# Cross-attention scores in TensorE's two row halves, from two fp32r parts, in a post-norm decoder kernel

## Chip, cores and metric

The kernel runs on one core of one Trainium2 chip. The metric is device time in microseconds for one execution, the median of the runs shown.

## What is computed

There are 64 batches of 128 tokens with 512 features. Each goes through self attention (16 heads of 32, rotary positions, causal mask), cross attention and a linear layer on fp8-quantised rows, each followed by a residual sum and a layer norm. Cross attention is the part that changes. It attends over features: its 8 heads split the 128 tokens into groups of 16, and each head has 512 x 512 scores over a contraction of only 16.

```python
def xattn(q, k, v):                       # q = x, k = v = context, each (64, 128, 512)
    qh = q.reshape(b * 8, 16, 512)
    kh = k.reshape(b * 8, 16, 512)
    vh = v.reshape(b * 8, 16, 512)
    qk = jnp.einsum('bdm,bdn->bmn', qh, kh) / sqrt(16)
    ret = jnp.einsum('bmn,bcn->bcm', softmax(qk), vh)
x = layernorm(x + self_attn(x))
x = layernorm(x + xattn(x, context, context))
x = layernorm(x + quantised(x) @ quantised(weight).T)
```

## The kernel before

Each batch passes six stages, and up to six batches are under way at once. The order of all steps on each engine in one slot (one batch's worth of steps) is written out by hand in five tables: `SP_STEPS`, `POOL_STEPS`, `ACT_STEPS`, `DVE_STEPS`, `PE_STEPS`. An entry `cross_scores:23@4` means step `cross_scores`, number 23, for the batch that is at stage 4. Each engine runs its table once a slot in that order, waits on semaphores where a step needs another engine, and never reorders steps. The tables unroll to 69 slots, with the middle ones in a loop over two slots.

A linear layer (`proj_q`, `proj_k`, `proj_v`, `proj_o`, `ffn`; L872) multiplies two fp32r parts of the input with two fp32r parts of the weights, three products of 128 rows by 512 columns in each of four chunks. ScalarE makes the high part `lin_h`, VectorE the low part `lin_l`.

Cross scores are computed twice. `cross_scores` (L985) writes a head's 128 x 512 block of scores with queries in rows into `mx`; VectorE's `cross_max` (L715) takes the negative row maximum. When 16 maxima of four heads (a group) are there, `cross_shift` splits them, `cross_shift_T` (L991) turns them, ScalarE copies them, and two small DMAs put them as rows 96 and 97 into `qst`. Then `cross_scores_T` (L1002) writes the block with keys in rows and with the maximum already subtracted into `st`, ScalarE's `probs` (L559) takes the exponential into `pp`, and `cross_pv` (L1014) multiplies it with the values of four heads, one in each 32-column group of the array, in plain fp32. `mx` and `st` have two banks each, used in turn, so TensorE can fill one while the other is read.

For precision, a head's 16 contraction rows are laid out several times. The query is split in two fp16 parts, the context in three bf16 parts, and five products of parts are stacked: 80 rows, padded with zeros to 96. ScalarE and GpSimd make the parts (`query_high`, `query_low`, `context_high`, `context_rest`), SyncE stores them to HBM (`st_qpl`, `st_kpl`) and loads them back head by head (`ld_qst`, `ld_kst`, five DMAs for each group of four heads).

A batch has 32 `cross_scores` and 32 `cross_scores_T`, one for each head and each block of 128. Three further PSUM banks serve all other products in turns (`BANK`).

## Time and profile before

| | before |
|---|---|
| median of 3 runs | 3355.27 us (3353.78 to 3358.29) |
| profiled execution: span from first to last instruction | 3353.3 us |
| TensorE busy | 3148.0 us, 94% |
| VectorE busy | 2792.0 us, 83% |
| ScalarE busy | 2093.1 us, 62% |
| GpSimd busy | 1251.8 us, 37% |
| moved by DMA | 220.66 MB, mean 66 GB/s |

The page gives the span as the profiled execution's own time and nothing that lies around it. PE is TensorE's matmuls, PEld its weight loads, DVE VectorE, ACT ScalarE, POOL GpSimd, SP SyncE.
### The profile page before, as it was taken

What the parts mean: (1) busy time and instruction counts of PE and PEld (TensorE: products, weight loads), DVE (VectorE), ACT (ScalarE), POOL (GpSimd) and SP (SyncE); (2) the same over time, 40 slices, a digit from 0 to 9 for tenths busy, and PEclk for the clock granted to TensorE, in tenths of its full rate; (3) what the DMA queues carried; (4) which work ended last, traced back from release to release, by engine and by line L of the source; (5) the groups of instructions that cost most, each with busy time, mean ns of one, the idle gap of its engine ahead of it and who ended that gap; (6) DMA issues with size and microseconds to landing.
All of it is one profiled execution on the core that took longest, in us unless ns stands there. A gap on an engine that the chain in (4) does not pass through costs nothing.

```text
span 3353.3 us, 79176 instructions
## 1 busy us (share of the span) xinstructions
PE 3148.0 (94%) x22224; PEld 1676.5 (50%) x22224; DVE 2792.0 (83%) x5187; ACT 2093.1 (62%) x3905; POOL 1251.8 (37%) x1623
## 2 busy tenths in 40 slices
PE   1689999999999999999999999999999999999986
PEld 1445555555555555555555555555555555555432
DVE  6368888888888888888888888888888888888874
ACT  0346666666676666666667666666666766666653
POOL 3223334334343333433433333343343433334321
PEclk9789999999999999999999999999999999999997
DMA  2022222222222222222222122222222222222220
GB/s 75 26 62 74 71 67 71 63 72 65 70 73 64 72 64 66 71 63 73 64 70 73 63 71 66 66 71 63 71 66 70 73 63 71 65 66 71 67 64 17
DMA packets 203973, 220.66 MB, mean 66 GB/s; under 512 B 37760, under 2 KB 160640, under 8 KB 203776
## 3 DMA queue, kind: packets, MB, share of 16 engines
q1 hardware_dynamic: 203776, 218.77, 21.4%
q14 instruction: 163, 1.34, 0.1%
q8 instruction: 34, 0.56, 0.1%
HBM read 141.57 MB, written 77.07 MB: 65 GB/s over the span
## 4 chain that ended last, share of the span: by engine, by line
PE 75%; DVE 14%; issue 7%; POOL 2%; ACT 1%; DVEq 1%; DMA 1%; SPq 0%; POOLq 0%; ACTq 0%
PE bank L872 19%; PE mx L985 14%; PE st L1002 13%; PE pv L1014 12%; PE bank L865 5%; PE bank L907 3%; DVE nm L715 3%; PE bank L956 3%; DVE st L776 2%; PE bank L939 2%; PE bank L959 2%; DVE lin_l L743 1%; DVE yout L838 1%; PE bank L923 1%; PE bank L920 1%
## 5 line engine op out<-in xcount | busy, mean ns | idle before, releaser
L715 DVE TENSOR_REDUCE nm<-mx 128x1 f32<-128x512 f32 x2048 | 1355.0, 685 | 219.9 <-PE mx L985 210.2
L559 ACT ACTIVATE pp<-st 128x512 f32<-128x512 f32 x2048 | 1153.0, 597 | 400.9 <-PE st L1002 385.1
L985 PE MATMUL mx<-kst,qst 96*128 96x512 bf16 x2048 | 765.4, 387 | 29.2 <-DVE nm L715 28.8
L1002 PE MATMUL st<-qst,kst 98*128 98x512 f16 x2048 | 739.6, 387 | 6.9 <-DMA qst<-cross_shift 2.6
L1014 PE MATMUL pv<-pp,vT 128*32 128x512 f32 x4096 | 551.2, 610 | 0.0
L985 PEld LDWEIGHTS mx<-kst,qst 96*128 96x128 f16 x2048 | 189.1, 98 | 445.5 <-DVE nm L715 283.1
L872 PE MATMUL bank<-w_h,lin_h 128*128 128x512 f32 x768 | 394.0, 513 | 4.5 <-DVE lin_l L743 4.4
L1002 PEld LDWEIGHTS st<-qst,kst 98*128 98x128 bf16 x2048 | 190.7, 98 | 317.8 <-ACT pp L559 216.6
L490 POOL TENSOR_SCALAR rstd<-mv 128x1 f32<-128x1 f32 x192 | 36.9, 192 | 817.2 <-DVE mv L779 812.1
L872 PE MATMUL bank<-w_l,lin_h 128*128 128x512 f32 x768 | 306.0, 398 | 0.0
L872 PE MATMUL bank<-w_h,lin_l 128*128 128x512 f32 x768 | 305.0, 397 | 0.0
L500 POOL TENSOR_TENSOR qkn<-ropeA,qkn 128x512 f16<-128x512 f32 x128 | 148.4, 1159 | 397.2 <-ACT qkn L581 391.4
L763 DVE RECIPROCAL o<-bank 128x128 f32<-128x128 f32 x256 | 217.1, 910 | 42.8 <-PE bank L959 42.7
L506 POOL TENSOR_SCALAR_AFFINE_SELECT p<-p 128x512 f32<-128x512 f32 x256 | 163.4, 638 | 197.8 <-ACT p L616 197.7
L496 POOL TENSOR_TENSOR ropeA<-ropeA,ropeB 128x512 f32<-128x512 f32 x128 | 163.7, 1279 | 144.9 <-DVE ropeB L755 144.9
L574 ACT ACTIVATE junk<-bank 128x512 bf16<-128x512 f32 x128 | 76.1, 594 | 203.3 <-PE bank L872 203.3
L616 ACT ACTIVATE p<-bank 128x512 f32<-128x512 f32 x256 | 152.6, 596 | 56.1 <-PE bank L939 47.4
L729 DVE TENSOR_REDUCE nm<-bank 128x4 f32<-128x512 f32 x256 | 174.6, 683 | 10.4 <-PE bank L923 10.3
L568 ACT ACTIVATE lin_h<-bank 128x512 fp32r<-128x512 f32 x64 | 38.2, 597 | 221.1 <-PE bank L865 221.1
L907 PE MATMUL bank<-ident,qkn 128*96 128x128 f16 x2048 | 161.9, 223 | 14.4 <-DVE o L763 7.2
L872 PEld LDWEIGHTS bank<-w_h,lin_h 128*128 128x128 f32 x768 | 149.4, 195 | 44.8 <-DVE lin_l L743 5.9
L907 PEld LDWEIGHTS bank<-ident,qkn 128*96 128x96 f16 x2048 | 146.0, 125 | 48.4 <-issue 19.3
(131 smaller groups left out, 5417.6 us busy)
## 6 DMA issues: line engine op xcount, KB each, us to landing
qst<-q_planes SPq DMA_DIRECT2D x640, 64.0 KB, 2.2
kst<-k_planes SPq DMA_DIRECT2D x640, 64.0 KB, 2.2
k_planes<-kpl SPq DMA_DIRECT2D x64, 384.0 KB, 2.6
xb<-x SPq DMA_DIRECT2D x64, 256.0 KB, 2.7
cx<-ctx SPq DMA_DIRECT2D x64, 256.0 KB, 3.3
q_planes<-qpl SPq DMA_DIRECT2D x64, 256.0 KB, 2.2
x_rows<-x SPq DMA_DIRECT2D x64, 256.0 KB, 2.1
x<-x_rows SPq DMA_DIRECT2D x64, 256.0 KB, 2.7
```

The lines of the kernel that those rows point to most:

```text
L496: g_.tensor_tensor(ropeA[:], ropeA[:], ropeB[:], ALU.add).then_inc(s_rope, 1)
L506: g_.affine_select(out=p1[c % 2][:], in_=p1[c % 2][:], compare_op=ALU.is_ge, fill=0.0, base=0, pattern=[[0, HC], [1, P]], channel_multipli ...
L559: a.activation(pp[:, unit % 2, j, :], st[n % 2][:], ACT.Exp, scale=CROSS_SCALE).then_inc(st_free, 1)
L715: v.tensor_reduce(nm2[:, n // 16, n % 16:n % 16 + 1], mx[n % 2][:], AX.X, ALU.max, negate=True)\
L729: v.tensor_reduce(nm1[:, HC * c:HC * (c + 1)], at(f"s1m{c}")[:].rearrange("p (h k) -> p h k", h=HC), AX.X, ALU.max, negate=True).then_inc( ...
L763: v.reciprocal(o1[:, cols], at("pvs")[:, cols]).then_inc(done, 1)
L865: last = t.transpose(dst[:, c * P:(c + 1) * P], src(c), idm[:])
L872: last = t.matmul(at(name)[:], a[:, rows], w[:, part, cols], start=(part == 0 and i == 0), stop=(part == KC - 1 and i == 2))
L907: last = t.transpose(at(name)[0:SROWS, h * P // 2:(h + 1) * P // 2].bitcast(F16), qkn[k][:, 8 * (i % 2) + h, :, :].rearrange("p g d -> p ( ...
L985: t.matmul(mx[n % 2][:], qst[b.i][0:XROWS, h, c * P:(c + 1) * P], kst[b.i][0:XROWS, h, :], start=True, stop=True).then_inc(mx_full, 1)
L1002: t.matmul(st[n % 2][:], kst[b.i][:, h, i * P:(i + 1) * P], qst[b.i][:, h, :], start=True, stop=True).then_inc(st_full, 1)
L1014: last = t.matmul(pv[32 * j:32 * j + 2 * XD, :], vT[b.i][:, i, GH * g + j, :], pp[:, unit % 2, j, :], start=(i == 0), stop=(i == KC - 1))
```

## The change

Query and context are now both split into two fp32r parts, and three products of parts are stacked: 48 rows for a head. `qst` and `kst` have 128 rows: one head of a pair stands in rows 0 to 47 (two shift rows at 48 and 49), the next in rows 64 to 111 (shift rows 112 and 113). `cross_scores` and `cross_scores_T` are 16 steps each instead of 32, and each issues two matmuls, one for each half of the array's rows, into the two banks of `mx` or `st`. One reduction and one exponential read both banks, 1024 elements. There is one `mx` and one `st` now, not two in turn. The scaling of the maxima goes, the shifts and their transpose are fp32r and fp32, `context_rest` becomes one subtraction, the planes in HBM are 4 bytes wide, the loads are six DMAs a group, and the ones beside the values take one column in place of 16. All five tables and the assignment of banks are new. Since `ffn`, `proj_q` and `proj_o` follow each other in another order, the steps that write `lin_h` wait until the linear layer before has been multiplied (`linear_before`).

```diff
+    ROW_TILE, PAIRS = 64, XH // 2
     NEG = -1e30
     SROWS = 3 * HD
-    XROWS = 96
-
-    Q_PLANE, K_PLANE = (0, 0, 0, 1, 1), (0, 1, 2, 0, 1)
-    N_SC = XH * KC
+    Q_PLANE, K_PLANE = (0, 0, 1), (0, 1, 0)
+    XROWS = len(Q_PLANE) * XD
+    PG = PAIRS // GROUPS
+    N_SC = PAIRS * KC
...
-        qpl = sb("qpl", [P, 2, D], F16)
-        kpl = sb("kpl", [P, 3, D], BF16)
-        qst = [sb(f"qst{i}", [XROWS + 2, XH, D], F16) for i in range(2)]
-        kst = [sb(f"kst{i}", [XROWS + 2, XH, D], BF16) for i in range(2)]
-        vT = [sb(f"vT{i}", [P, KC, XH, 2 * XD]) for i in range(2)]
+        qpl = sb("qpl", [P, 2, D], F32R)
+        kpl = sb("kpl", [P, 2, D], F32R)
+        qst = [sb(f"qst{i}", [P, PAIRS, D], F32R) for i in range(2)]
+        kst = [sb(f"kst{i}", [P, PAIRS, D], F32R) for i in range(2)]
+        vT = [sb(f"vT{i}", [P, KC, XH, XD + 1]) for i in range(2)]
...
-        st = [bank(f"st{i}") for i in range(2)]
+        st = es.enter_context(nc.psum_tensor("st", [P, 2, 512], F32))
         pv = bank("pv")
-        mx = [bank(f"mx{i}") for i in range(2)]
+        mx = es.enter_context(nc.psum_tensor("mx", [P, 2, 512], F32))
         banks = [bank(f"bank{i}") for i in range(3)]
...
         DVE_STEPS = steps("""
+            cross_max:6@4 cross_max:7@4 layernorm:2@6 cross_shift:0@4 cross_norm:0@5 cross_max:8@4
+            self_recip:0@2 self_recip:1@2 cross_max:9@4 self_recip:2@2 self_recip:3@2
+            self_norm:0@2 cross_max:10@4 oT_low:0@2 cross_norm:1@5 cross_max:11@4 add_cross:0@5
+            cross_max:12@4 layernorm:1@5 quant_scale:0@5 cross_max:13@4 self_max:0@1
+            quant_magic:0@5 add_self:0@2 cross_max:14@4 self_max:1@1 self_max:2@1 cross_max:15@4
+            self_max:3@1 xdT_low:0@5 layernorm:0@2 self_shift:0@1 cross_max:0@3 cross_shift:1@4
+            xT_low:0@0 cross_max:1@3 add_ffn:0@5 cross_max:2@3 cross_max:3@3 rope_terms:0@0
+            cross_max:4@3 cross_max:5@3 rope_terms:1@0""")
...
         PE_STEPS = steps("""
-            proj_o:3@2 context_T:0@3 cross_scores_T:5@4 cross_scores_T:6@4 cross_pv:0@4
-            cross_scores_T:7@4 parts_T:3@1 cross_scores_T:8@4 cross_scores:23@4 self_scores:0@1
-            cross_scores_T:9@4 cross_pv:1@4 cross_scores_T:10@4 cross_scores:24@4 cross_scores:25@4
-            cross_scores_T:11@4 self_scores:1@1 cross_scores_T:12@4 cross_scores:26@4 self_scores:2@1
-            cross_scores:27@4 cross_scores_T:13@4 cross_scores_T:14@4 cross_scores:28@4 quant_T:0@5
-            cross_scores:29@4 cross_scores_T:15@4 cross_pv:2@4 cross_scores:30@4 cross_scores:31@4
-            ffn:0@5 ffn:1@5 ffn:2@5 ffn:3@5 x_T:0@0 cross_shift_T:1@4 cross_scores:0@3 cross_pv:3@4
-            self_scores:3@1 cross_scores:1@3 proj_q:0@0 proj_q:1@0 proj_q:2@0 proj_q:3@0
-            cross_scores:2@3 proj_k:0@0 proj_k:1@0 self_shift_T:0@1 proj_k:2@0 cross_scores:3@3
-            proj_k:3@0 cross_scores_T:16@4 cross_scores:4@3 proj_v:0@0 cross_scores_T:17@4
-            cross_scores:5@3 cross_scores_T:18@4 cross_scores:6@3 proj_v:1@0 cross_scores:7@3
-            proj_v:2@0 cross_scores:8@3 cross_scores_T:19@4 cross_scores:9@3 cross_scores_T:20@4
-            proj_v:3@0 self_scores_T:0@1 cross_pv:4@4 cross_scores:10@3 self_scores_T:1@1
-            cross_scores_T:21@4 cross_scores:11@3 cross_scores_T:22@4 self_scores_T:2@1
-            cross_scores:12@3 self_pv:0@1 cross_scores:13@3 cross_scores_T:23@4 self_pv:1@1
-            self_scores_T:3@1 cross_scores:14@3 cross_scores_T:24@4 cross_scores:15@3
-            cross_scores_T:25@4 self_pv:2@1 parts_T:0@0 self_pv:3@1 cross_scores_T:26@4
-            cross_scores_T:27@4 cross_pv:5@4 cross_shift_T:0@3 cross_scores_T:28@4 cross_scores_T:29@4
-            group_T:0@4 cross_scores_T:30@4 cross_scores:16@3 cross_scores_T:31@4 cross_pv:6@4
-            cross_scores:17@3 cross_pv:7@4 cross_scores:18@3 cross_scores:19@3 parts_T:1@0 group_T:1@4
-            proj_o:0@1 cross_scores:20@3 cross_scores_T:0@3 cross_scores_T:1@3 back_T:0@4 parts_T:2@0
-            proj_o:1@1 cross_scores_T:2@3 cross_scores:21@3 proj_o:2@1 cross_scores_T:3@3
-            cross_scores:22@3 cross_scores_T:4@3""")
+            group_T:1@5 cross_scores:11@4 back_T:0@5 context_T:0@3 cross_scores_T:0@4 parts_T:1@1
+            parts_T:2@1 cross_scores:12@4 proj_o:0@2 proj_o:1@2 cross_scores_T:1@4 proj_o:2@2
+            cross_scores:13@4 cross_scores_T:2@4 self_scores:0@1 proj_o:3@2 parts_T:3@1
+            cross_scores_T:3@4 cross_pv:0@4 self_scores:1@1 cross_scores:14@4 self_scores:2@1
+            cross_scores_T:4@4 cross_pv:1@4 self_scores:3@1 cross_scores:15@4 cross_scores_T:5@4
+            quant_T:0@5 cross_scores_T:6@4 cross_scores:0@3 x_T:0@0 ffn:0@5 ffn:1@5
+            self_shift_T:0@1 ffn:2@5 ffn:3@5 cross_scores:1@3 cross_scores_T:7@4 cross_shift_T:1@4
+            cross_pv:2@4 proj_q:0@0 proj_q:1@0 cross_scores:2@3 proj_q:2@0 proj_q:3@0
+            self_scores_T:0@1 proj_k:0@0 cross_scores:3@3 cross_pv:3@4 cross_scores_T:8@4
+            proj_k:1@0 cross_scores:4@3 proj_k:2@0 proj_k:3@0 cross_scores_T:9@4 self_scores_T:1@1
+            proj_v:0@0 cross_scores:5@3 proj_v:1@0 proj_v:2@0 proj_v:3@0 cross_scores_T:10@4
+            self_scores_T:2@1 cross_scores:6@3 cross_pv:4@4 self_pv:0@1 cross_scores_T:11@4
+            self_pv:1@1 cross_scores:7@3 self_scores_T:3@1 cross_scores_T:12@4 group_T:0@4
+            cross_scores:8@3 self_pv:2@1 cross_scores_T:13@4 self_pv:3@1 cross_shift_T:0@3
+            cross_pv:5@4 cross_scores_T:14@4 cross_scores:9@3 parts_T:0@0 cross_scores_T:15@4
+            cross_pv:6@4 cross_scores:10@3 cross_pv:7@4""")
...
+        def linear_before(name, b):
+
+            opens = [(i, stage, turn) for i, (step, k, stage) in enumerate(PE_STEPS) if k == 0
+                     for first, turn in LINEARS if step == first]
+            own = [turn for _, _, turn in opens].index(name)
+            for back in range(1, len(opens) + 1):
+                _, stage, turn = opens[own - back]
+                ahead = opens[own][1] - stage - (back > own)
+                if b.rnd is not None or 0 <= b.b + ahead < BATCH:
+                    return [full(turn, b, ahead)]
+            return []
...
-                    sp.dma_start(kst[b.i][r * XD:(r + 1) * XD, GH * g:GH * (g + 1), :],
-                                 kpl_d[b.idx()][K_PLANE[r]][GH * g * XD:GH * (g + 1) * XD, :]
-                                 .rearrange("(h d) n -> d h n", d=XD)).then_inc(d_kst[b.i][g], 16)
+                for q in range(2):
+                    for r in range(3):
+                        row = ROW_TILE * q + r * XD
+                        sp.dma_start(kst[b.i][row:row + XD, PG * g:PG * (g + 1), :].bitcast(F32),
+                                     kpl_d[b.idx()][K_PLANE[r]].rearrange("(p q d) n -> q d p n", q=2, d=XD)
+                                     [q][:, PG * g:PG * (g + 1), :]).then_inc(d_kst[b.i][g], 16)
...
+            def context_low(b, _):
+                pool.wait_ge(s_kh, b.n(1, 1))
+                g_.tensor_tensor(kpl[:, 1, :], cx[:], kpl[:, 0, :].bitcast(F32), ALU.subtract).then_inc(s_kl, 1)
...
             def probs(b, n):
 
-                unit, j = n // GH, n % GH
+                unit, j = n // PG, 2 * (n % PG)
                 act.wait_ge(st_full, b.n(N_SC, n + 1))
                 act.wait_ge(pv_unit, b.n(UNITS, unit - 1))
-                a.activation(pp[:, unit % 2, j, :], st[n % 2][:], ACT.Exp, scale=CROSS_SCALE).then_inc(st_free, 1)
+                a.activation(pp[:, unit % 2, j:j + 2, :], st[:], ACT.Exp, scale=CROSS_SCALE).then_inc(st_free, 1)
...
             def xT_high(b, _):
+                for point in linear_before("v", b):
+                    act.wait_ge(*point)
                 act.wait_ge(*full("xT", b))
...
             def cross_max(b, n):
                 dve.wait_ge(mx_full, b.n(N_SC, n + 1))
-                v.tensor_reduce(nm2[:, n // 16, n % 16:n % 16 + 1], mx[n % 2][:], AX.X, ALU.max, negate=True)\
-                 .then_inc(mx_free, 1)
+                p, c = n // KC, n % KC
+                out2 = nm2[:, p // PG, :].rearrange("m (q l c) -> m q l c", q=2, l=PG)[:, :, p % PG, c]
+                v.tensor_reduce(out2, mx[:], AX.X, ALU.max, negate=True).then_inc(mx_free, 1)
 
             def cross_shift(b, g):
 
-                dve.wait_ge(mx_free, b.n(N_SC, 16 * (g + 1)))
-                v.tensor_scalar(nm2[:, g, :], nm2[:, g, :], 1.0 / SHIFT_UNIT, None, ALU.mult).then_inc(s_sc2, 1)
-                dve.wait_ge(s_sc2, b.n(GROUPS, g + 1))
+                dve.wait_ge(mx_free, b.n(N_SC, N_SC // GROUPS * (g + 1)))
                 v.tensor_copy(sh2[:, g, 0, :], nm2[:, g, :]).then_inc(s_h2, 1)
                 dve.wait_ge(s_h2, b.n(GROUPS, g + 1))
-                v.tensor_tensor(sh2[:, g, 1, :], nm2[:, g, :], sh2[:, g, 0, :], ALU.subtract).then_inc(s_sh2, 1)
+                v.tensor_tensor(sh2[:, g, 1, :], nm2[:, g, :], sh2[:, g, 0, :].bitcast(F32), ALU.subtract)\
+                 .then_inc(s_sh2, 1)
...
             def cross_scores(b, n):
 
-                h, c = n // KC, n % KC
-                if n % (GH * KC) == 0:
-                    pe.wait_ge(d_kst[b.i][h // GH], b.n2(80, 80))
-                    pe.wait_ge(d_qst[b.i][h // GH], b.n2(80, 80))
-                pe.wait_ge(mx_free, b.n(N_SC, n - 1))
-                t.matmul(mx[n % 2][:], qst[b.i][0:XROWS, h, c * P:(c + 1) * P], kst[b.i][0:XROWS, h, :],
-                         start=True, stop=True).then_inc(mx_full, 1)
+                p, c = n // KC, n % KC
+                if n % (PG * KC) == 0:
+                    pe.wait_ge(d_kst[b.i][p // PG], b.n2(96, 96))
+                    pe.wait_ge(d_qst[b.i][p // PG], b.n2(96, 96))
+                pe.wait_ge(mx_free, b.n(N_SC, n))
+                for q in range(2):
+                    rows = slice(ROW_TILE * q, ROW_TILE * q + XROWS)
+                    last = t.matmul(mx[:, q, :], qst[b.i][rows, p, c * P:(c + 1) * P], kst[b.i][rows, p, :],
+                                    start=True, stop=True)
+                last.then_inc(mx_full, 1)
 
             def cross_shift_T(b, g):
                 pe.wait_ge(s_sh2, b.n(GROUPS, g + 1))
                 pe.wait_ge(*before(f"mT{g}", b))
-                t.transpose(at(f"mT{g}")[0:32, 0:P // 2].bitcast(F16), sh2[:, g].rearrange("p a h -> p (a h)"),
-                            ident16[:]).then_inc(bank_full[BANK[f"mT{g}"]], 1)
+                t.transpose(at(f"mT{g}")[0:32, 0:P], sh2[:, g].rearrange("p a h -> p (a h)").bitcast(F32),
+                            ident[:]).then_inc(bank_full[BANK[f"mT{g}"]], 1)
 
             def cross_scores_T(b, n):
 
-                unit, j = n // GH, n % GH
+                unit, p = n // PG, n % PG
                 g, i = unit // KC, unit % KC
-                h = GH * g + j
-                if n % (GH * KC) == 0:
-                    pe.wait_ge(d_sh2[g], b.n(16, 16))
-                pe.wait_ge(st_free, b.n(N_SC, n - 1))
-                t.matmul(st[n % 2][:], kst[b.i][:, h, i * P:(i + 1) * P], qst[b.i][:, h, :],
-                         start=True, stop=True).then_inc(st_full, 1)
+                p += PG * g
+                if n % (PG * KC) == 0:
+                    pe.wait_ge(d_sh2[g], b.n(32, 32))
+                pe.wait_ge(st_free, b.n(N_SC, n))
+                for q in range(2):
+                    rows = slice(ROW_TILE * q, ROW_TILE * q + XROWS + 2)
+                    last = t.matmul(st[:, q, :], kst[b.i][rows, p, i * P:(i + 1) * P], qst[b.i][rows, p, :],
+                                    start=True, stop=True)
+                last.then_inc(st_full, 1)
 
             def cross_pv(b, unit):
 
                 g, i = unit // KC, unit % KC
-                pe.wait_ge(st_free, b.n(N_SC, GH * (unit + 1)))
+                pe.wait_ge(st_free, b.n(N_SC, PG * (unit + 1)))
                 if unit == 0:
                     pe.wait_ge(*freed("vT", b))
                 if i == 0:
                     pe.wait_ge(pv_free, b.n(GROUPS, g))
                 for j in range(GH):
-                    last = t.matmul(pv[32 * j:32 * j + 2 * XD, :], vT[b.i][:, i, GH * g + j, :],
+                    last = t.matmul(pv[32 * j:32 * j + XD + 1, :], vT[b.i][:, i, GH * g + j, :],
                                     pp[:, unit % 2, j, :], start=(i == 0), stop=(i == KC - 1))
                 last.then_inc(pv_unit, 1)
```

## Rows read from the trace of the kernel before

**Rows 1.** The page: busy time, and the granted clock in 40 slices.

```profile
PE 3148.0 (94%) x22224; PEld 1676.5 (50%) x22224; DVE 2792.0 (83%) x5187; ACT 2093.1 (62%) x3905; POOL 1251.8 (37%) x1623
PEclk9789999999999999999999999999999999999997
```

**Rows 2.** Windows: start:end, length, busy us (instructions) by engine, clock, DMA share, GB/s.

```profile
1501.00:1549.56 48.56, 48.08 (x350) 25.95 (x348) 42.91 (x81) 32.55 (x62) 19.13 (x26) 1.00 0.22 69
...
500.00:1500.00 1000.00, 979.03 (x7021) 522.31 (x7023) 867.16 (x1622) 662.51 (x1238) 388.11 (x508) 1.00 0.22 68
```

**Rows 3.** Groups by line and shape, weight loads: count, busy us, mean ns, idle before.

```profile
L985 PEld LDWEIGHTS mx<-kst,qst 96*128 96x128 f16 x2048 | 189.1, 98 | 445.5 <-DVE nm L715 283.1 <-issue 120.0
...
L872 PEld LDWEIGHTS bank<-w_h,lin_h 128*128 128x128 f32 x768 | 149.4, 195 | 44.8 <-DVE lin_l L743 5.9
...
L1014 PEld LDWEIGHTS pv<-pp,vT 128*32 128x32 f32 x4096 | 81.0, 108 | 151.1 <-issue 107.4 <-ACT pp L559 37.5
```

**Rows 4.** Timeline, TensorE, score matmuls in a row: start us, duration us.

```profile
1523.72 0.38 PE L985 MATMUL mx<-kst,qst 96*128 96x512 bf16 x1
...
1523.94 0.38 PE L1002 MATMUL st<-qst,kst 98*128 98x512 f16 x1
```

**Rows 5.** Timeline, TensorE, around `cross_pv`; first a window with its first four records.

```profile
1529.94 0.64 PE L1014 MATMUL pv<-pp,vT 128*32 128x512 f32 x4
...
1529.63 0.39 PE L1002 MATMUL st<-qst,kst 98*128 98x512 f16 x1
1529.94 1.06 PE L1014 MATMUL pv<-pp,vT 128*32 128x512 f32 x8
1530.94 0.39 PE L985 MATMUL mx<-kst,qst 96*128 96x512 bf16 x1
```

**Rows 6.** Timeline, TensorE, `self_shift_T` and the projection behind it.

```profile
1511.68 0.22 PE L930 MATMUL bank<-ident,sh 128*32 128x128 f16 x1 [0.48 <-DVE sh L739]
1511.84 0.50 PE L872 MATMUL bank<-w_h,lin_h 128*128 128x512 f32 x1
1512.18 0.39 PE L872 MATMUL bank<-w_l,lin_h 128*128 128x512 f32 x1
1512.41 0.40 PE L872 MATMUL bank<-w_h,lin_l 128*128 128x512 f32 x1
```

**Rows 7.** Groups by line and shape, ScalarE and VectorE: busy us, mean ns.

```profile
L600 ACT ACTIVATE qs<-bank 96x1024 f16<-96x1024 f16 x128 | 130.5, 1020 | 47.5 <-PE bank L907 47.5
...
L784 DVE TENSOR_SCALAR yout<-yout,mv,rstd 128x512 f32<-128x512 f32 x64 | 85.6, 1338 | 31.1 <-POOL rstd L492 31.1
...
L802 DVE TENSOR_TENSOR yq<-bank,r 128x256 f32<-128x256 f32 x128 | 54.4, 425 | 9.2
...
L809 DVE TENSOR_TENSOR x<-bank,x 128x512 f32<-128x512 f32 x64 | 44.3, 692 | 28.5 <-PE bank L865 28.3
```

**Rows 8.** Timeline, VectorE and ScalarE in the same slot.

```profile
1524.14 1.29 DVE L715 TENSOR_REDUCE nm<-mx 128x1 f32<-128x512 f32 x2 [0.65 <-PE mx L985]
...
1526.55 3.39 DVE L763 RECIPROCAL o<-bank 128x128 f32<-128x128 f32 x4 [0.49 <-PE bank L959]
...
1531.37 0.69 DVE L715 TENSOR_REDUCE nm<-mx 128x1 f32<-128x512 f32 x1 [0.30 <-PE mx L985]
...
1532.69 0.78 DVE L773 TENSOR_TENSOR lin_l<-o,lin_h 128x512 fp32r<-128x512 f32 x1
...
1535.80 0.69 DVE L809 TENSOR_TENSOR x<-bank,x 128x512 f32<-128x512 f32 x1 [0.51 <-PE bank L865]
...
1537.49 1.29 DVE L715 TENSOR_REDUCE nm<-mx 128x1 f32<-128x512 f32 x2
...
1528.49 2.16 ACT L559 ACTIVATE pp<-st 128x512 f32<-128x512 f32 x4
```

**Rows 9.** Waits: who waited for whom, us in total, times, longest.

```profile
PEld pv L1014 <- issue: 107.4, 357, 0.8
```

**Rows 10.** DMA issues: queue, count, KB each, us to landing.

```profile
qst<-q_planes SPq DMA_DIRECT2D x640, 64.0 KB, 2.2
```

125 lines of the change are left out of this document (55 added, 70 removed), and 6 rows, old and new, of the table BANK.

## The prediction

> **What bounds the kernel now.** I read the page first for the busy shares and the granted clock [rows 1]. TensorE is busy 94% of the span and VectorE 83%, and the digits stay level from the third of the 40 slices on, so one steady slot decides. The windows give that slot [rows 2]: 48.56 us, with TensorE busy 48.08 us of it, VectorE 42.91 and ScalarE 32.55. Over a longer stretch TensorE is idle 21 us in 1000, one in each slot of 48.56. The granted clock is 1.00 there (2.4 GHz). TensorE's queue is the bound, and a change is worth what it takes off or puts on that queue, less the idle time that it fills or opens. VectorE stands close behind.
>
> Next I laid out TensorE's slot by start-to-start times. Two score matmuls in a row are 0.22 us apart [rows 4]; inside a projection they are 0.23 us apart [rows 6]. Per slot: 64 score matmuls at 0.22, 14.1 us; 60 fp32r matmuls at 0.23, 13.9; 8 `cross_pv` of 0.88, 7.1; the rest (24 fp32 transposes, parts, self scores, `self_pv`, shifts) 9.1. That is 44.2 us. What is missing to 48.56 are switches of the array's tiling, 2.8 us, worked out below, and waits of about 1.6.
>
> **The saving in matmuls.** The 64 score matmuls become 32 pairs. Whether the two halves of a pair run together, the trace doesn't show for row halves. It does for column quarters: four `cross_pv` matmuls in the array's four column groups, each recorded at about 0.6 us, end 0.64 us after the first began [rows 5]. I take a pair as one fp32r matmul, 0.24 us. Removed 64 x 0.22 = 14.1, added 32 x 0.24 = 7.7, two shift transposes in fp32 +0.1: **-6.3 us** a slot. The other end, halves that run one after the other, is 64 x 0.23 = 14.7, +0.6. I take the low end because the nearest row is another split of the same array.
>
> **The cost in switches.** A score matmul before has 96 or 98 rows, and it follows a projection in the same tiling. Now it uses a half of 64 rows, while its neighbours use all 128. What does such a switch cost? From a score matmul to `cross_pv` it is 0.31 us where the next of a kind comes after 0.22: 0.09 on entry. `cross_pv` takes 1.00 us to the next score matmul [rows 5]; its eight records are two passes of 0.43, plus three offsets of 0.007 each, so 0.10 is left for the way out. The weight loads on either side are 0.11 and 0.10 us long [rows 3], and loads don't run ahead of the switch: TensorE's loads wait 107 us in all ahead of `pv` for "issue" [rows 9]. The third case is dearer. `self_shift_T` has 32 columns, so it is in the column tiling, and a projection follows it [rows 6]: it starts at 1511.68, the projection's first matmul at 1511.84, the second at 1512.18. A 128-column transpose takes 0.06 and a projection matmul 0.23, together 0.29, and here they take 0.50: **0.21** for a switch into fp32r weights, whose load is recorded at 0.19 us against 0.10 for 16-bit ones [rows 3]. So the price of a switch is close to the length of the first weight load behind it.
>
> I counted the switches in `PE_STEPS`, cyclically. Before: 14 into the column tiling and 14 out of it, 13 of these to 16-bit work and one to fp32r: 14 x 0.09 + 13 x 0.10 + 0.21 = 2.8 us. After: 60. Into the row halves 27 (the 32 pairs stand in 27 groups), at 0.20 since their weights are now fp32r: 5.4. Into full-width fp32 or fp32r work 13 x 0.20 = 2.6, into full-width 16-bit work 9 x 0.10 = 0.9, into the column tiling 11 x 0.09 = 1.0. Sum 9.9, so **+7.1 us**. Bounds: if only the draining counted, 0.10 everywhere, 60 x 0.10 = 6.0 and the sum is +3.2; if a switch between full width and row halves were free, only the column tiling's 22 stay (11 in, 1.0; 11 out, 9 of them to fp32r at 0.20, 2.0) and the sum is +0.2; if the second half's weights are loaded after the first's, up to 0.19 more for each of 27, +12.2. The nearest row is the projection behind `self_shift_T`, the same number format and width, and I take it.
>
> The Trainium skill (TensorEngine Tiling, Key Properties) states that changing the tiling mode, not only the tile, drains the engine, and speaks so against this change; the trace agrees for the column tiling with its 0.09 to 0.21 us [rows 5, 6], and for the row halves no row shows it. The same skill (TensorE: Matmul & The Clock Gate, Part 3) puts a group of row tiles at one matmul's time plus some 4 ns a tile, by which a pair would be 0.24 us as well.
>
> TensorE's work is then 47.0 - 6.3 + 7.1 = **47.8 us** a slot, 0.8 more than before.
>
> **The new waits.** `mx` and `st` were two buffers each; now each is one buffer of two banks, and TensorE may not write pair n+1 until pair n has been read. VectorE's two reductions of 512 take 0.60 us each start to start (1.29 for two, less one of 0.69) [rows 8]. By operations of 256 and 512 elements out of the same banks, 425 and 692 ns [rows 7], an element is 1.04 ns, so one of 1024 is 1.13 start to start and 1.22 to its end. The reduction starts 0.43 us after its matmul [rows 5, 8]; with 0.1 for the exposed load and 0.1 to hand back, the loop is 1.85 us. ScalarE: four exponentials in 2.16 us, 0.52 each [rows 8], and a 1024-element copy is 1.02 [rows 7], so the loop of `st` is 1.65 us. Laying TensorE's work between pairs out in the new order, the loop is longer than it at `cross_scores` 15 to 0 (1.56 us), and at `cross_scores_T` 1 to 2 (1.58), 5 to 6 (1.08) and 14 to 15 (1.23): 0.3 and 1.1 us of wait. VectorE's own queue adds to this. From `cross_max` 7 to 12 it holds five reductions (5.7 us), `layernorm:2` 1.3, four reciprocals 3.3, `self_norm` and `oT_low` 1.3, two `cross_norm` 1.4, `add_cross` 1.7 [rows 7, 8]: 14.7 us. TensorE's work between the same pairs is 12.5, and with one buffer it can't run ahead; some 2 us are lost there. These stretches lie partly under one another, and slack behind one takes up the next: I take **2.6 us** of waits in place of 1.6. If nothing is taken up it is 3.8.
>
> **What costs nothing.** VectorE: 32 x 0.60 - 16 x 1.13 = 1.1 less, two scalings 0.4 less, so about 41 us a slot, under TensorE's 50. ScalarE: 32 x 0.5 - 16 x 0.94, one context copy 0.5 less; it falls to about 31. GpSimd loses one of two context subtractions. TensorE hides all three; without it VectorE would be next. DMA: 24 loads of 64 KB for 20, stores of 512 KB and 512 for 384 and 256, about 0.65 MB more on 3.42 MB a batch, at a busy share of 22% [rows 2]; a load lands in 2.2 us [rows 10]. If a load were late, the first pair of a group would wait for it. The 17 columns of `vT` for 32 change no matmul's moving length. The new waits of `xT_high` and `oT_high` for the linear before them protect one `lin_h`: between `ffn` and `proj_q` TensorE has 1.9 us of other work, and the copy and subtraction take as long. The stage numbers are higher, but TensorE still runs from stage 0 to 5, so fill and drain keep their length.
>
> **The sum.** 47.8 + 2.6 = 50.4 us a slot against 48.56, +1.85; times 64 batches, +118 us. The profiled execution's span is 3353.3 us, and the page gives no time around it; the runs' median of 3355.27 stands 2.0 above. 3353.3 + 118 + 2 = **3473 us**, slower.
>
> **The rivals.**
> - *Row halves switch without a drain.* Then TensorE has 40.9 us of work and VectorE 41; where two reductions follow each other (2 and 3, 4 and 5, 6 and 7) or a buffer is late one waits for the other, some 4.5 us. Slot 45.5, 64 x -3.1: **3160 us**, faster. It is one mechanism: the price of entering the halves. For it speaks that no row shows a row switch; against it all three column cases. It decides below 0.1 us a switch. 0.20.
> - *Drain only, 0.10 a switch.* Work 43.9, waits 3.7 since TensorE now runs into VectorE's stretch: 47.6, **3290 us**. Against it speaks the 0.21 of the projection. 0.17, of which a quarter within or above no change.
> - *The pair's two weight loads follow each other* before either half is full, 0.1 to 0.19 more at 27 entries, part of it hidden in waits: slot 52.2 to 54, **3590 to 3700 us**. 0.14.
> - *The halves don't overlap:* 32 x 0.23 = +7.4 and a slot near 57.5, **3930 us**. 0.04.
> - The forecast 0.42, with its own range of 3400 to 3550; 0.03 for what I didn't see.
>
> The range of 3140 to 3640 leaves out half of the first rival, the top of the third and the fourth. A difference under 0.2% is about what a measurement of this kernel can't tell from no change. Faster 0.33, same 0.05, slower 0.62.
>
> **What the profile after would show.** A score pair's two matmuls within 0.02 us of each other say that the halves run together; the next matmul 0.4 us behind an isolated pair says that a switch costs what I say, 0.25 us that it is free. The slot is right at about 50.4 us, TensorE's loads in front of pairs should wait on "issue", and TensorE should wait for `nm` at pairs 8 to 12. The prediction is wrong if switches into the halves are cheap, or if VectorE's reduction of 1024 is far from 1.13 us.

## The result and the profile after

| | before | after |
|---|---|---|
| median of 4 runs | 3355.31 us (3353.78 to 3358.29) | 3510.78 us (3505.57 to 3553.53) |
| ratio, 95% interval | | 1.0489 (1.0434 to 1.0544) |
| profiled execution | span 3353.3 us | 3505.57 us, span 3503.8 us |
| steady slot, mean | 49.34 us | 51.74 us |

The change makes the kernel slower by 4.9%, 155 us. The forecast was slower, 3473 us; the measured time is 38 us above it and inside the range. The slot's length is the distance between two starts of `self_shift_T`, taken over the steady slots of one execution (between about 400 and 2900 us).

The page of the kernel after, its busy times, its granted clock, and the groups of the score path:

```profile
PE 3181.2 (91%) x22224; PEld 1682.0 (48%) x22224; DVE 2636.7 (75%) x4036; ACT 1958.9 (56%) x2817; POOL 1179.3 (34%) x1557
...
PEclk9789999999999999999999999999999999999987
...
L725 DVE TENSOR_REDUCE nm<-mx 128x2 f32<-128x1024 f32 x1024 | 1249.2, 1220 | 543.0 <-PE mx L995 532.8
L564 ACT ACTIVATE pp<-st 128x1024 f32<-128x1024 f32 x1024 | 1045.1, 1021 | 557.4 <-PE st L1015 555.9
L1015 PE MATMUL st<-qst,kst 50*128 50x512 f32 x2048 | 505.3, 490 | 74.6 <-ACT pp L564 71.6
...
L995 PE MATMUL mx<-kst,qst 48*128 48x512 f32 x2048 | 507.4, 492 | 14.2 <-DVE nm L725 13.9
L1015 PEld LDWEIGHTS st<-qst,kst 50*128 50x128 f32 x2048 | 195.1, 187 | 356.1 <-issue 163.5
```

Against [rows 1] VectorE, ScalarE and GpSimd each have less to do, and TensorE's share fell to 91%, though its slot grew. TensorE is still the engine on which the slot is spent, but it idles more. The one slot of [rows 2] has this counterpart in the windows of the kernel after (start:end, length, busy us and instructions by engine, clock, DMA share, GB/s):

```profile
1611.36:1662.78 51.42, 48.58 (x348) 25.66 (x347) 40.47 (x63) 30.50 (x44) 18.25 (x24) 1.00 0.24 78
500.00:1500.00 1000.00, 943.42 (x6705) 499.22 (x6706) 784.60 (x1204) 592.47 (x851) 351.32 (x462) 0.99 0.25 78
```

TensorE is idle 2.84 us of this slot, against 0.48 us of the slot of [rows 2], and 57 us in 1000 against 21, which is 2.9 us a slot against 1.0. The timeline of TensorE names the places, always by the same rows from slot to slot; here they stand with what surrounds a pair in three settings (start us, duration us, then idle time before the row and who ended it):

```profile
1502.25 0.50 PE L995 MATMUL mx<-kst,qst 48*128 48x512 f32 x2
1502.59 0.40 PE L1015 MATMUL st<-qst,kst 50*128 50x512 f32 x2
...
1504.11 0.50 PE L1015 MATMUL st<-qst,kst 50*128 50x512 f32 x2 [0.53 <-ACT pp L564]
...
1511.89 0.39 PE L880 MATMUL bank<-w_h,lin_l 128*128 128x512 f32 x1
1512.21 0.50 PE L995 MATMUL mx<-kst,qst 48*128 48x512 f32 x2
1512.64 0.50 PE L880 MATMUL bank<-w_h,lin_h 128*128 128x512 f32 x1
1512.98 0.40 PE L880 MATMUL bank<-w_l,lin_h 128*128 128x512 f32 x1
...
1526.84 0.50 PE L1015 MATMUL st<-qst,kst 50*128 50x512 f32 x2
1527.27 0.43 PE L964 MATMUL bank<-p,va 128*32 128x128 f32 x8
...
1529.44 0.66 PE L873 MATMUL bank<-ident,o 128*128 128x128 f32 x4 [0.34 <-ACT p L623]
...
1534.92 0.49 PE L1015 MATMUL st<-qst,kst 50*128 50x512 f32 x2 [0.38 <-ACT pp L564]
...
1538.69 0.65 PE L873 MATMUL bank<-ident,o 128*128 128x128 f32 x4 [0.87 <-ACT o L569]
...
1540.48 0.66 PE L873 MATMUL bank<-ident,yq 128*128 128x128 f32 x4 [0.72 <-DVE yq L810]
```

Three things are to be seen. A pair's two matmuls are one row of 0.50 us where a single one is recorded at 0.49: the halves run together. The next matmul starts 0.43 us behind an isolated pair (1512.21 to 1512.64, 1526.84 to 1527.27) and 0.34 behind one that another pair follows. And the waits are five: for `st` twice (before `cross_scores_T` 6 and 15), for ScalarE's `p` before `group_T:0`, for its copy `o` before `group_T:1`, and for VectorE's `yq` before `back_T`.

By start-to-start times the slot of 51.43 us, which is one without a fall of the clock (below), is 37.7 of matmuls, 3.3 of waits (the idle time above and about 0.1 for the load that follows each wait), and what is left, 10.4, of switches and exposed loads.

The clock adds a little. In the windows of the kernel after, around the last two waits of that list:

```profile
1538.00:1541.00 3.00, 1.60 (x11) 1.13 (x12) 2.84 (x5) 1.07 (x2) 0.97 (x1) 1.00 0.77 219
1541.10:1544.50 3.40, 3.40 (x25) 2.49 (x23) 1.93 (x4) 2.35 (x3) 0.74 (x2) 0.50 0.58 189
```

The granted clock is 1.00 (2.4 GHz) in the first window, in which TensorE is busy 1.60 of 3.00 us, and 0.50 (1.2 GHz) in the second, of 3.4 us. Between 400 and 2900 us there are eight such stretches, 34 us in all, and none in the kernel before. The slots that hold one last 52.9 or 54.4 us in place of 51.4. That lifts the mean slot by 0.3 us. Most slots have the same waits and no fall, so the waits alone don't decide it. The stretches fit the spread of the runs as well: the one of 3553.53 us has a mean clock of 0.957 against 0.973 of the profiled one.

### The profile page after: what moved, and what is told of

Same layout as the page of the kernel before. It is cut to its first block, busy times and chain, and to the rows that moved or that the text cites. A ratio compares the mean times of both kernels' runs of the same rounds, so it can differ in the third digit from the quotient of the medians.

```text
span 3503.8 us, 73683 instructions
## 1 busy us (share of the span) xinstructions
PE 3181.2 (91%) x22224; PEld 1682.0 (48%) x22224; DVE 2636.7 (75%) x4036; ACT 1958.9 (56%) x2817; POOL 1179.3 (34%) x1557
## 4 chain that ended last, share of the span: by engine, by line
PE 81%; ACT 6%; issue 3%; DVE 2%; SPq 0%; DMA 0%; ACTq 0%; POOL 0%; DVEq 0%; POOLq 0%
PE bank L880 28%; PE pv L1028 14%; PE st L1015 11%; PE mx L995 10%; PE bank L873 4%; ACT pp L564 4%; PE bank L915 3%; PE bank L964 2%; PE bank L928 2%; PE bank L947 2%; PE bank L931 2%; PE bank L967 2%; ACT p L623 1%; ACT lin_h L630 1%; PE bank L1002 1%
## 5 line engine op out<-in xcount | busy, mean ns | idle before, releaser
L725 DVE TENSOR_REDUCE nm<-mx 128x2 f32<-128x1024 f32 x1024 | 1249.2, 1220 | 543.0 <-PE mx L995 532.8
L564 ACT ACTIVATE pp<-st 128x1024 f32<-128x1024 f32 x1024 | 1045.1, 1021 | 557.4 <-PE st L1015 555.9
L1015 PE MATMUL st<-qst,kst 50*128 50x512 f32 x2048 | 505.3, 490 | 74.6 <-ACT pp L564 71.6
L1028 PE MATMUL pv<-pp,vT 128*17 128x512 f32 x4096 | 549.0, 608 | 0.4 <-ACT pp L564 0.3
L995 PE MATMUL mx<-kst,qst 48*128 48x512 f32 x2048 | 507.4, 492 | 14.2 <-DVE nm L725 13.9
L1015 PEld LDWEIGHTS st<-qst,kst 50*128 50x128 f32 x2048 | 195.1, 187 | 356.1 <-issue 163.5
L880 PE MATMUL bank<-w_h,lin_h 128*128 128x512 f32 x768 | 349.7, 455 | 9.0 <-DVE lin_l L751 8.3
L995 PEld LDWEIGHTS mx<-kst,qst 48*128 48x128 f32 x2048 | 195.0, 186 | 279.1 <-issue 225.8
L771 DVE RECIPROCAL o<-bank 128x128 f32<-128x128 f32 x256 | 224.7, 920 | 10.4 <-PE bank L967 10.4
L520 POOL TENSOR_TENSOR kpl<-cx,kpl 128x512 fp32r<-128x512 f32 x64 | 82.3, 1287 | 341.5 <-ACT kpl L640 341.5
L491 POOL TENSOR_SCALAR rms<-ssq 128x1 f32<-128x1 f32 x128 | 24.3, 190 | 510.5 <-ACT junk L581 510.2
```

The costliest lines, as they stand in the source:

```text
L564: a.activation(pp[:, unit % 2, j:j + 2, :], st[:], ACT.Exp, scale=CROSS_SCALE).then_inc(st_free, 1)
L725: v.tensor_reduce(out2, mx[:], AX.X, ALU.max, negate=True).then_inc(mx_free, 1)
L771: v.reciprocal(o1[:, cols], at("pvs")[:, cols]).then_inc(done, 1)
L880: last = t.matmul(at(name)[:], a[:, rows], w[:, part, cols], start=(part == 0 and i == 0), stop=(part == KC - 1 and i == 2))
L995: last = t.matmul(mx[:, q, :], qst[b.i][rows, p, c * P:(c + 1) * P], kst[b.i][rows, p, :], start=True, stop=True)
L1015: last = t.matmul(st[:, q, :], kst[b.i][rows, p, i * P:(i + 1) * P], qst[b.i][rows, p, :], start=True, stop=True)
```

## The experiments

All times are against the kernel before on the same chip (medians 3353.18 to 3356.59 us); slots are means over the steady ones. First the parts of the change, each undone in the kernel after.

**Full rows.** Both matmuls of a pair run over all 128 rows, one after the other, still fp32r.

```diff
-                    rows = slice(ROW_TILE * q, ROW_TILE * q + XROWS)
+                    rows = slice(0, P)
...
-                    rows = slice(ROW_TILE * q, ROW_TILE * q + XROWS + 2)
+                    rows = slice(0, P)
```

> The changed kernel with every score matmul over all 128 rows of the array in place of a half, so both banks get the sum of two heads (the rows behind each head's 48 hold zeros; the shift rows have weight zero and the exponential a scale 10,000 times smaller, so that it stays finite: this part of the output is not the reference's). The same number of matmuls, reductions, exponentials, waits and steps. Theory (the halves run together, and entering and leaving them costs about as much as that saves): 32 matmuls of 0.233 us more in a slot, +7.5 us, and the tiling price falls from about 10.4 us to 3.0, -7.4: within 0.6 us of the changed kernel's 51.4 us a slot, 3470 to 3550 us. Rival (switches into the halves are cheap, and the loss comes from the single buffers): +7 us a slot, 3900 us or more.

Measured: 3584.0 us, ratio 1.068 (1.0662 to 1.0698), slot 53.04. That is 73 us over the kernel after, so the halves are worth 1.3 to 1.6 us a slot (against the mean of 51.74 or the 51.43 of its undisturbed slots), far from the 7.5 that they save in matmuls. The time is 34 us above the range that I had expected and far below the rival's 3900. The timeline of this kernel shows why, beside a projection and then among the column tiling's work:

```profile
1500.43 0.39 PE L881 MATMUL bank<-w_h,lin_l 128*128 128x512 f32 x1
1500.65 0.63 PE L996 MATMUL mx<-kst,qst 128*128 128x512 f32 x2
1501.12 0.40 PE L881 MATMUL bank<-w_h,lin_h 128*128 128x512 f32 x1
1501.35 0.40 PE L881 MATMUL bank<-w_l,lin_h 128*128 128x512 f32 x1
...
1505.62 0.40 PE L968 MATMUL bank<-p,ones 128*32 128x128 f32 x8
1505.95 0.73 PE L1016 MATMUL st<-qst,kst 128*128 128x512 f32 x2
1506.61 0.43 PE L965 MATMUL bank<-p,va 128*32 128x128 f32 x8
```

From the last projection matmul before the pair to the second one behind it are 1500.43 to 1501.35, 0.92 us: four matmuls of 0.23 and no switch. The same distance with row halves is 1511.89 to 1512.98, 1.09 us: three matmuls' worth, 0.70, and 0.39 for going in and out. **So beside a projection a pair in halves is 0.17 us dearer than two matmuls over all rows, with fp32r.** Among the column tiling's work, where a switch is due either way, it is cheaper: 0.43 against 0.66.

**16-bit scores.** The score matmuls read only the upper 16 bits of each part.

```diff
+            def view(part):
+                return part.bitcast(BF16).rearrange("r (n two) -> r n two", two=2)[:, :, 1]
...
-  t.matmul(mx[:, q, :], qst[b.i][rows, p, c * P:(c + 1) * P], kst[b.i][rows, p, :],
+  t.matmul(mx[:, q, :], view(qst[b.i][rows, p, c * P:(c + 1) * P]), view(kst[b.i][rows, p, :]),
```

> The changed kernel with the score matmuls reading the upper 16 bits of the same fp32r words as bf16 (scores of lower precision, so the output is not the reference's). Theory (the price of a switch is mostly the length of the first weight load behind it, 0.10 us for 16-bit weights against 0.19 for fp32r): each of 32 pairs loses about 0.09 us of exposed load and 0.016 us of matmul, 3.4 us a slot on TensorE, of which waits take back up to 1: the median falls by 150 to 220 us, to 3290 to 3360 us. Rival (the price is the drain of the array alone): 0.5 us a slot, 3480 us.

Measured: 3396.3 us, ratio 1.0131 (1.0103 to 1.0158); slot 49.35 undisturbed, 49.86 with 58 us at half clock. 114 us less than the kernel after. The group of its weight loads for `mx`, by line and shape:

```profile
L999 PEld LDWEIGHTS mx<-kst,qst 48*128 48x128 bf16 x2048 | 100.4, 94 | 292.2 <-issue 171.5 <-DVE nm L725 94.3
```

A load is 94 ns in place of 187. The timeline has the place of 1512.21 again:

```profile
1518.30 0.40 PE L999 MATMUL mx<-kst,qst 48*128 48x512 bf16 x2
1518.63 0.50 PE L880 MATMUL bank<-w_h,lin_h 128*128 128x512 f32 x1
```

The projection behind the lone pair starts after 0.33 us in place of 0.43, though its own weights are fp32r as before. So it is the pair's own load that the format changes, 0.10 us for each of 32 pairs, 3.2 us in all. The undisturbed slot falls by 2.1 (51.43 to 49.35); the rest goes into waits, of which TensorE's idle time shows a part, 64 us in 1000 for 57. The length of the first load behind a switch is therefore part of the price, as the prediction had it, but the time is above the 3290 to 3360 us that I expected.

**Full rows and 16-bit scores.** Both edits at once: this leaves of the change only the rest, which is the pairing of heads, the single buffers, the other parts and DMAs, and the new order.

> The kernel of e1_full_rows (all score matmuls over 128 rows; both banks get the sum of two heads, shift weights zero, exponential scale 10,000 times smaller) with the score operands read as bf16, so each score matmul is the one that the kernel before has, in time and tiling. What is left of the change is the new order, one buffer of two banks for each kind of score, and readers of 1024 elements. Theory (these parts cost nothing net; the loss lies in the row halves): 44.0 us of matmuls, 2.3 of switches and 3.3 of waits, 49.6 us a slot, 3350 to 3420 us, the kernel before within 2%. Rival (single buffers and the order are the loss): 3480 us or more.

Measured: 3493.92 us, ratio 1.041 (1.0393 to 1.0428), slot 51.67. My expectation fell and the rival held. With the score matmuls back at full width and 16 bits, 138 of the 155 us are still lost. The halves and fp32r together come to 17 us, and not even to that in the slot: 51.67 us stands beside 51.43 of the undisturbed slots of the kernel after, while this kernel has no fall of the clock between 400 and 2900 us. Its window says where the time is:

```profile
500.00:1500.00 1000.00, 930.60 (x6584) 486.19 (x6700) 785.41 (x1203) 591.41 (x850) 351.88 (x462) 1.00 0.26 78
```

TensorE is idle 69 us in 1000, 3.6 a slot, for 1.0 before. Its waits are at the same five places as in the kernel after. Taken with the two kernels above, row halves are a gain in both formats, 73 us with fp32r (3584.0 to 3510.8) and 98 with 16 bits (3493.9 to 3396.3); fp32r is the loss beside it, 90 us over full rows and 114 in halves.

**Readers of half length.** VectorE and ScalarE read 512 elements of the two banks instead of 1024.

```diff
-  a.activation(pp[:, unit % 2, j:j + 2, :], st[:], ACT.Exp, scale=CROSS_SCALE)
+  a.activation(pp[:, unit % 2, j, :], st[:, 0, :], ACT.Exp, scale=CROSS_SCALE)
...
-  v.tensor_reduce(out2, mx[:], AX.X, ALU.max, negate=True)
+  v.tensor_reduce(out2, mx[:, :, 0:256], AX.X, ALU.max, negate=True)
```

> The changed kernel with the readers of the score banks halved: each maximum reads 256 of the 512 columns of each bank, each exponential one bank of two, and the value matmuls use that bank's probabilities for both heads (the other half of the maxima and of the exponentials is left out). TensorE's work is the same. It shortens the loop of a single buffer from about 1.85 to 1.3 us and frees VectorE and ScalarE. Theory (waits for the single buffers are 1 to 2 us of a slot, the switches the rest): -60 to -130 us, 3380 to 3450 us. Rival (the single buffers are the whole loss): below 3360 us.

Measured: 3458.19 us, ratio 1.0302 (1.0284 to 1.0319); slot 50.6 undisturbed. 52 us less, and 8 above the range that I had expected. The two waits for `st` are gone from the timeline (9.6 us of them are left in the execution, of 71.6), and of the other three, which stay, two are:

```profile
1579.02 0.65 PE L873 MATMUL bank<-ident,o 128*128 128x128 f32 x4 [0.88 <-ACT o L569]
1580.82 0.66 PE L873 MATMUL bank<-ident,yq 128*128 128x128 f32 x4 [0.72 <-DVE yq L810]
```

So the slow readers are about a third of the loss. The edit shortens them and at the same time frees VectorE and ScalarE, so it doesn't tell the single buffer from the engines' own time. The other waits are where the new order puts a step too close behind the one that it needs.

**Fewer switches by pairing the pairs.** TensorE's table places each `cross_scores` beside a `cross_scores_T` where it can: 43 switches for 60. It also moves `context_T` and `back_T`, away from two of the waits.

```diff
-  cross_scores_T:6@4 cross_scores:0@3 x_T:0@0 ffn:0@5 ffn:1@5
-  self_shift_T:0@1 ffn:2@5 ffn:3@5 cross_scores:1@3 cross_scores_T:7@4
+  cross_scores:0@3 cross_scores_T:5@4 x_T:0@0 ffn:0@5 ffn:1@5 self_shift_T:0@1 ffn:2@5
+  cross_scores:1@3 cross_scores_T:6@4 ffn:3@5
```

> The changed kernel with TensorE's order alone rewritten: every cross_scores stands beside a cross_scores_T, so the 32 pairs stand in 16 groups in place of 27 and there are 43 switches in place of 60; context_T stands before group_T:1, and cross_scores:11 and cross_scores_T:0 between group_T:1 and back_T, where TensorE waits in the changed kernel. Theory: the tiling price falls from 10.4 to 8.6 us a slot and the two waits at group_T:1 and back_T from 1.7 to about 0.3: 48.5 us a slot if no new wait comes, 3320 us; with new waits up to 3420. Rival (the order was balanced and a different one opens waits that cost as much): 3500 us or more.

Measured: 3875.81 us, ratio 1.1544 (1.1525 to 1.1564), slot 57.79. The theory fell: what seventeen switches save is lost several times over in waits. TensorE is idle 150 us in 1000. In its timeline the largest wait of a slot is new:

```profile
1542.63 0.49 PE L880 MATMUL bank<-wf_h,lin_h 128*128 128x512 f32 x1 [1.83 <-DVE lin_l L840]
```

**Orders against the waits.** Two kernels of the same work whose TensorE table takes the steps behind the five waits elsewhere. Both move `cross_pv:7` behind `context_T` and `group_T:1` later still, and two steps of `proj_o` ahead of `back_T`; the first also gathers some pairs (47 switches against the second's 54) and moves one ScalarE step.

```diff
-  group_T:1@5 cross_scores:11@4 back_T:0@5 context_T:0@3 cross_scores_T:0@4 parts_T:1@1
+  context_T:0@3 cross_pv:7@5 cross_scores_T:0@4 cross_scores:11@4 group_T:1@5 proj_o:0@2
+  proj_o:1@2 back_T:0@5 parts_T:1@1 cross_scores:12@4
```

> The changed kernel, complete, with a new order of TensorE's steps and one step of ScalarE moved (self_shift_out behind xT_high). The 32 pairs stand in 22 groups with 47 switches in place of 27 and 60; between the steps where TensorE waits in the changed kernel other work is put (cross_scores_T:0 and cross_scores:11 and two steps of proj_o around group_T:1, self_scores:3 behind quant_T, self_pv:2 ahead of group_T:0, cross_pv:6 ahead of cross_scores_T:15). Theory: tiling price 10.4 to 8.6 us a slot, waits 3.3 to about 1.5: 47.9 us, 3270 us, up to 3350 with some new waits; faster than the kernel before. Rival (each new order opens waits of its own, as the sixteen groups did): above 3450 us.

> The same moves away from TensorE's waits as in e6_order, with the score pairs and self_shift_T left where the changed kernel has them: 54 switches, of which the tiling price is 9.6 us a slot. Theory: 10.4 to 9.6 us of switches and 3.3 to about 1.5 of waits: 48.8 us, 3330 us, up to 3400. The distance to e6_order is the price of 7 switches, about 1 us a slot or 60 us.

Measured: 3665.39 us, ratio 1.0924 (1.0904 to 1.0943), and 3638.24 us, ratio 1.0851 (1.083 to 1.0872); slots 54.4 and 53.9. Both expectations fell, and the seven switches fewer brought nothing either: the first kernel is the slower one. One wait is common to both. TensorE in the first kernel, then SyncE's queue, the time that the issuing of a DMA takes:

```profile
1543.27 0.79 PE L1015 MATMUL st<-qst,kst 50*128 50x512 f32 x2 [2.92 <-DMA qst<-cross_shift]
```

```profile
1535.11 0.35 SPq L421 DMA_DIRECT2D cross_shift<-sh2T  x1
1535.83 2.89 SPq L388 DMA_DIRECT2D kst<-k_planes  x6
...
1540.45 0.74 SPq L430 DMA_DIRECT2D qst<-cross_shift  x2
```

`cross_scores_T:0` now comes earlier, and the two shift DMAs that it needs stand in SyncE's queue behind the six loads of `ld_kst:0`, whose issuing takes 2.89 us. It waits 2.92 us for them. Such waits come to 183.1 us of the execution in the first kernel and 175.8 in the second, which covers what the slots have grown by (2.7 and 2.1 us, 64 times). In the kernel after they come to 3.0 us: the six DMAs are hidden, but with little to spare.

**The order mended.** From here on `ld_kst:0` stands behind `ld_sh2:0` in SyncE's table, `context_T` ahead of `group_T:1`, `cross_scores_T:0` ahead of `back_T`, `self_scores:3` behind `quant_T`, and `group_T:0` one pair later. 57 switches are left of 60.

```diff
-  st_sh2:0@5 ld_kst:0@4 ld_x2r:0@6 st_out:0@7 ld_sh2:0@5 ld_kst:1@4
+  st_sh2:0@5 ld_x2r:0@6 st_out:0@7 ld_sh2:0@5 ld_kst:0@4 ld_kst:1@4
...
-  group_T:1@5 cross_scores:11@4 back_T:0@5 context_T:0@3 cross_scores_T:0@4 parts_T:1@1
+  context_T:0@3 group_T:1@5 cross_scores:11@4 cross_scores_T:0@4 back_T:0@5 parts_T:1@1
...
-  self_scores_T:3@1 cross_scores_T:12@4 group_T:0@4 cross_scores:8@3 self_pv:2@1
+  self_scores_T:3@1 cross_scores_T:12@4 self_pv:2@1 cross_scores:8@3 group_T:0@4
```

> The changed kernel, complete, with small moves only. TensorE: context_T ahead of group_T:1, cross_scores:11 and cross_scores_T:0 between group_T:1 and back_T, self_scores:3 behind quant_T, self_pv:2 ahead of group_T:0. SyncE: the six loads of ld_kst:0 go behind ld_sh2:0; in the changed kernel they stand ahead of it and hold the shift rows back by 2.9 us, which made e6_order and e7_waits wait 3 us a slot at cross_scores_T:0. Theory (those runs lost by that queue and by proj_o moved ahead of its input, not by their other moves): waits fall from 3.3 us a slot to about 1.5, the tiling price by 0.3: 49.4 us a slot, 3360 to 3420 us. Rival (any other order loses): 3520 us or more.

Measured: 3448.2 us, ratio 1.0281 (1.0264 to 1.0298), slot 50.72, alike in every slot, no half clock between 400 and 2900 us. 62 us less than the kernel after with the same work, but above the 3360 to 3420 us that I expected. 45 of them are the slot (51.43 to 50.72, 64 times), and the rest goes with the stretches at half clock. Queue and order were moved together, and what each is worth alone wasn't run.

Two more kernels keep this order. One gathers pairs for five fewer switches, the other has full rows and 16-bit scores.

> e9_order with five fewer switches: cross_scores:2 behind cross_pv:2, cross_scores:4 beside cross_scores_T:9, cross_scores_T:10 beside cross_scores:6. By the prices read after the change (0.1 us into the halves, 0.2 out of them to fp32r work) the tiling price falls by 0.7 us a slot: 45 us below e9_order if no wait opens. Rival (the moved pairs wait for their buffers or delay a reader): at or above e9_order.

> The kernel of e8_full_16bit (score matmuls over all 128 rows as bf16, sums of two heads, shift weights zero, exponential scale 10,000 times smaller) with the order of e9_order on TensorE and SyncE. Theory (e8 lost 2.4 us a slot against the kernel before by the waits of its order, 4.5 us in place of 2.4, and not by its matmuls or switches): 1.5 to 2 us a slot less than e8, 3370 to 3400 us. Rival (single buffers and readers of 1024 elements cost it whatever the order): 3470 us or more.

Measured: 3457.68 us, ratio 1.0311 (1.0293 to 1.0328), slot 50.69; and 3440.57 us, ratio 1.0261 (1.0244 to 1.0278), slot 50.77. The first is what its rival said, and the second missed its 3370 to 3400 us. The five switches bought nothing in the slot (the 9 us by which this kernel is slower lie outside the steady slots). In the kernel with five fewer switches TensorE waits where it did not before:

```profile
1589.13 0.50 PE L995 MATMUL mx<-kst,qst 48*128 48x512 f32 x2 [0.77 <-DVE nm L725]
```

The chain that ended last, for the kernel with the mended order, leaves TensorE here:

```profile
1610.44 0.60 PE bank L873 x4
...
1612.92 1.07 DVE o L771 x2
...
1615.77 1.68 DVE o L771 x2
...
1621.63 0.69 DVE x L817
...
1622.36 0.65 PE bank L915 x8
```

From `group_T:0` at 1610.44 to `parts_T:2` at 1622.36 the chain runs through VectorE: reductions, four reciprocals, `cross_norm`, `add_cross`. TensorE's own work beside this stretch is not what sets its length. I took that for the cause of the three equal slots and made one more order.

**VectorE's stretch shortened.** `layernorm:2` is done ahead of `cross_max:7` and so leaves the stretch; `group_T:0` goes back to its place. The same with 16-bit scores.

```diff
-  cross_max:6@4 cross_max:7@4 layernorm:2@6
+  cross_max:6@4 layernorm:2@6 cross_max:7@4
```

> The changed kernel, complete, with the order of e9_order on TensorE and SyncE except that group_T:0 is back in its place ahead of cross_scores:8, and with layernorm:2 between cross_max:6 and 7 on VectorE in place of behind 7. e9_order, e10_merged and e11_full16_order all had a slot of 50.7 us though their matmuls and switches differ by up to 7 us, and their chain passes VectorE from cross_max:7 to add_cross without a gap. Theory (that stretch of VectorE, with TensorE's work from back_T round to cross_scores:7, closes the slot): layernorm:2 takes 0.85 us there, and VectorE idles 1.6 us ahead of cross_max:7, so the slot falls by 0.8 to 49.9 us, 3390 to 3410 us. Rival (TensorE's own sum is the bound): 3440 to 3450 us as e9_order.

> e12_vector with the score matmuls reading the upper 16 bits as bf16, as in e2_16bit (scores of lower precision). Theory: some 13 pairs lie in the TensorE part of the closing chain, each 0.1 us shorter: 1.3 us a slot below e12_vector, 48.6 us, 3300 to 3340 us, faster than the kernel before. Rival (VectorE alone closes the slot): within 20 us of e12_vector.

Measured: 3458.49 us, ratio 1.03 (1.028 to 1.032), slot 50.84; and 3329.36 us, ratio 0.9929 (0.9913 to 0.9946), slot 48.89. The first missed: no gain (`group_T:0` moved as well, so `layernorm:2` isn't tested alone). But its chain is another one. Where the kernel above is on VectorE, it reads:

```profile
1613.45 0.98 PE pv L1028 x8
...
1614.98 1.03 ACT pp L564
1616.06 0.49 PE st L1015 x2
...
1617.97 1.03 PE pv L1028 x8
...
1619.62 0.61 ACT lin_h L630
```

VectorE has only the last pieces, from 1620.25 to 1623.35. One reading is that two paths of nearly the same length lie side by side, one over VectorE and one over TensorE with its waits for ScalarE; the one taken away, the other stands there. The second kernel of the pair, in which TensorE's work is shorter by the 16-bit loads, fits it: 1.95 us a slot and 129 us. But the shorter loads gave as much in the first order (2.1 us a slot, down to 49.35) with VectorE's table untouched, so the two paths are argued and not shown. This kernel beats the kernel before by 0.7% (ratio 0.9913 to 0.9946), by scores of lower precision; at the precision of the kernel after, the mended order is the best, 2.8% slower than before. What else holds the slot at 50.7 to 50.8 I didn't separate further.

## Why the prediction was right, and where it was off

**Halves together: right.** The pair's group is 0.50 us long. The Trainium skill (TensorE: Matmul & The Clock Gate, Part 3) has a few ns a tile for it, and the trace agrees: 0.50 us for the pair against 0.49 for one. Matmuls are 37.7 us a slot after, 44.2 before: -6.5 for -6.3.

**The price of a switch: right, with one term missing.** The total was forecast at 9.9 us and is 10.4. Into the halves it is about 0.1 (0.32 to 0.33 from a projection matmul that takes 0.23), but 0.10 of the pair's own load lies open behind, and leaving costs 0.1 more, with a further 0.10 at the first projection matmul: 0.39 for the round trip, where I had 0.40. What I hadn't counted is a pair behind a pair in the same halves: 0.33 to 0.34, not 0.24, though nothing is switched. That is five times 0.10, the 0.5 us by which the total is off. The rule cited ahead, that changing the tiling mode drains the engine (the Trainium skill, TensorEngine Tiling, Key Properties), agrees with these rows for row halves: about 0.1 us at each way in and out beyond the exposed loads.

**The saving in matmuls is given back at the switches: right, and more fully than forecast.** This was the heart of the forecast, -6.3 and +7.1, so +0.8 us a slot on TensorE. Against the forecast's own 2.8 us of switches before, the 10.4 would be +7.6. But those 2.8 were counted and not read. Of the mean slot before, 49.34 us, 5.1 are left beside the matmuls, and only about 1.3 of them are waits (1.0 idle, and 0.1 for the load behind each of two or three waits); I estimate switches and exposed loads before at 3.8 from that. Then it is -6.5 and +6.6: TensorE's own work hardly changed. Two experiments differ from the kernel after by one aspect: against full rows in fp32r the halves gain 1.3 to 1.6 us, and fp32r in halves costs 2.1 over 16 bits. Full rows and 16 bits end within 17 us of the kernel after.

**The waits: right in kind, half of their growth, and partly at other places.** I took 2.6 us after and 1.6 before, +1.0. By the idle time and the loads behind it they are 3.3 after and about 1.3 before, +2.0, nearly all of what the undisturbed slot grew by (51.43 for 49.34). The kernel with full rows and 16 bits says the same: without halves and without fp32r the idle time is still 3.6 us a slot. So the number came out near, and by luck in part: the forecast put too much on TensorE's work and too little on its waits. Of the four forecast places, 5 to 6 and 14 to 15 of `cross_scores_T` show (0.53 and 0.38 of idle time). VectorE's stretch from `cross_max:7` to 12 was forecast at 14.7 us and runs from 1632.75 to 1647.87, 15.1 us, with no gap over 0.3 us, but it doesn't end in waits for `nm`: TensorE waits for `nm` 14 us in the whole execution. I had put some 2 us of loss there, and 2.3 us of idle time lie there, but they fall on the transposes, `group_T:0`, `group_T:1` and `back_T`, for ScalarE's and VectorE's pieces in between. I had laid out the single buffers' loops and not the chains of the small steps that the new order had moved close together. VectorE's timeline in the kernel after, the stretch's ends and what `back_T` waits for:

```profile
1632.75 1.23 DVE L725 TENSOR_REDUCE nm<-mx 128x2 f32<-128x1024 f32 x1 [1.63 <-PE mx L995]
1633.89 0.93 DVE L792 TENSOR_SCALAR yout<-yout,mv,rstd 128x512 f32<-128x512 f32 x1
...
1644.37 0.42 DVE L810 TENSOR_TENSOR yq<-bank,r 128x256 f32<-128x256 f32 x1
...
1647.87 1.23 DVE L725 TENSOR_REDUCE nm<-mx 128x2 f32<-128x1024 f32 x1 [0.28 <-PE mx L995]
```

Behind a reduction of 1024 the next instruction starts 1.13 to 1.14 us later, as forecast.

**The base: wrong.** I took the slot of [rows 2] for all. Every second slot of the kernel before is near 50.1 us, and the mean is 49.34. VectorE is late at the loop's head there. Its timeline in the kernel before, and TensorE's row behind it:

```profile
1588.99 0.55 DVE L784 TENSOR_SCALAR x<-x,mv,rstd 128x512 f32<-128x512 f32 x1 [1.78 <-issue]
...
1590.78 0.69 DVE L791 TENSOR_TENSOR x<-bank,xb 128x512 f32<-128x512 f32 x1
```

```profile
1591.53 0.39 PE L920 MATMUL bank<-maskb,identb 128*128 128x512 bf16 x1 [0.40 <-DVE x L791]
```

In the kernel after nothing of the kind holds TensorE up; all its slots are alike but for the clock.

**The sum.** Forecast 50.4 against 48.56. Measured: +0.7 of waits, +0.5 of switches and -0.2 of matmuls make 51.4; the clock, which the forecast left at full speed, makes it 51.7. Before, +0.8 makes it 49.3. The step is then 2.4 us in place of 1.85; 0.55 over 64 slots are 35 of the 38 us by which the forecast was low. The errors in the slot after, 1.3 us, and in the slot before, 0.8, had partly cancelled, which was luck.

**What remains of the cause.** The 138 us that stay with full rows and 16 bits belong to the rest of the change, not to the row halves or fp32r. The slow readers (52 us by one experiment) and the order of steps with SyncE's queue (62 us, and 53 with full rows and 16 bits) are the parts shown; they overlap, and together they don't account for everything. Two buffers each for `mx` and `st` weren't tried: the two, `pv` and the three shared banks take eight banks as it is, and four more would be needed.

The rivals: free switching is excluded by the 0.43 behind a pair, which 16-bit loads only bring down to 0.33; drain only, too, by the 2.1 us that 16-bit loads give back. Loads of the two halves one after the other would have shown as 0.19 more at each entry, and halves that don't overlap as a row of 0.63 to 0.73, as with full rows.

## What to carry to other kernels

Splitting the array's rows saves a matmul only where the neighbours are split too, or where a switch of tiling is due anyway; between full-width fp32r matmuls the way in and out (0.39 us here) costs more than the matmul saved (0.23). Before trading two buffers for one wide one, lay out the loop of write, read and hand back against the work between two writes, and then follow each small step that the new order brings near its producer. When a reorder gains nothing, look at the chain that ended last before and after: if it has moved to another engine, a second path of nearly the same length may stand behind the first. And when a change alters formats and order at once, undo the formats alone: here that showed that 138 of 155 us were not theirs.

## What the hardware showed that I had not expected

- A load runs ahead of the matmuls between full-width matmuls (0.23 us apart at a recorded load of 0.19), but not wholly between two pairs in the same row halves: 0.33 apart with fp32r loads of 0.19.
- Six DMA issues in a row take SyncE 2.89 us, 0.48 each; in an order with less slack TensorE waited 2.92 us for two small DMAs queued behind them.
- The granted clock fell from 1.00 to 0.50 for 3.4 to 6.8 us at a time, 34 us of the 2500 between 400 and 2900 us in the kernel after, 270 in the first kernel that waited for DMAs, and none there in the mended order, nor with full rows.
